# Cross-attention and routed experts on one core: table products summed over constants, and four weight sums at other ticks

## The reference

```python
scores = einsum('bsd,bmd->bsm', layernorm(x), ctx) / sqrt(512)
attn = softmax(where(mask, scores, -1e30)); readout = attn @ ctx       # zero where no row is allowed
x = x + readout
h = layernorm(x)
p = softmax(h @ G); value, indices = top_k(p, 2)                       # 8 experts
out = sum over the two: value * ((silu(h @ gate_e.T) * (h @ up_e.T)) @ down_e.T + (h @ lora_A_e.T) @ lora_B_e.T)
x = x + out
```

## Time and profile before

| | |
|---|---|
| median of 3 runs | 500.96 us (500.02 to 501.46) |
| profiled execution, its own time | 501.44 us |
| its span, first to last instruction | 499.6 us |
| mean granted TensorE clock | 0.995 |
| busy: TensorE, VectorE, ScalarE, GpSimd | 97%, 87%, 76%, 60% |

### The profile page before, as it was taken

One profiled execution on the slowest core, in us unless ns is written; L12 is line 12 of the kernel. 1 busy time (PEld: TensorE's weight loads), 2 busy tenths in 40 slices (PEclk: granted clock), 3 DMA queues, 4 the chain that ended last, 5 costly groups with the idle time before them and its releaser, 6 DMA issues.

```text
span 499.6 us, 16211 instructions
## 1 busy us (share of the span) xinstructions
PE 486.7 (97%) x4040; PEld 433.1 (87%) x4040; DVE 436.5 (87%) x1678; ACT 381.0 (76%) x1076; POOL 300.0 (60%) x440
## 2 busy tenths in 40 slices
PE   8999999999999989999999999999999999999994
PEld 7788888888888878899998999999998999999993
DVE  5799999999999987889988999999887888888885
ACT  4788888888888988888888778777565666666662
POOL 4327777777777887757886444445544445444544
PEclk9999999999999999999999999999999999999998
DMA  8999999999999999999999999989999999999932
GB/s 300 392 369 403 397 405 389 400 386 360 394 405 375 403 333 287 362 376 412 409 413 408 412 410 387 354 341 367 418 412 417 417 416 416 416 414 416 382 155 85
DMA packets 64839, 187.52 MB, mean 375 GB/s; under 512 B 9582, under 2 KB 9710, under 8 KB 64752
## 3 DMA queue, kind: packets, MB, share of 16 engines
q1 hardware_dynamic: 43584, 118.62, 62.6%
q0 software_dynamic: 20800, 67.65, 34.0%
q10 hardware_dynamic: 368, 0.21, 0.2%
HBM read 112.46 MB, written 78.73 MB: 383 GB/s over the span
## 4 chain that ended last, share of the span: by engine, by line
PE 73%; DMA 9%; POOL 6%; issue 6%; DVE 2%; ACT 2%; SPq 1%; POOLq 1%; DVEq 0%; ACTq 0%
PE rd L539 12%; PE bank L539 12%; PE bank L481 11%; PE bank L383 8%; PE rd L557 6%; PE rd L558 6%; PE rd L423 4%; DMA z_own<-z_rows 4%; PE bank L362 3%; PE rd L424 3%; DMA z_rows<-z_own 3%; PE rd L546 3%; POOL x_rows L1232 2%; DMA x_sb<-in_x 2%; PE rd L396 2%
## 5 line engine op out<-in xcount | busy, mean ns | idle before, releaser
L679 ACT COPY hT<-bank 128x512 f32<-128x512 f32 x140 | 81.7, 583 | 26.3 <-PE bank L481 22.2
L1232 POOL DMA_INDIRECT x_rows<-xe x64 | 65.7, 1026 | 32.4 <-issue 27.1
L539 PE MATMUL rd<-wg_sb,hT 128*128 x560 | 80.3, 286 | 0.4 <-ACT hT L679 0.4
L539 PE MATMUL bank<-wg_sb,hT 128*128 x560 | 80.2, 286 | 0.0
L383 PE MATMUL bank<-cc_sb,xnT 128*128 128x136 f32 x512 | 80.1, 286 | 0.0
L539 PEld LDWEIGHTS rd<-wg_sb,hT 128*128 128x128 f32 x560 | 72.6, 190 | 0.7 <-issue 0.7
L539 PEld LDWEIGHTS bank<-wg_sb,hT 128*128 128x128 f32 x560 | 72.6, 190 | 0.1
L383 PEld LDWEIGHTS bank<-cc_sb,xnT 128*128 128x128 f32 x512 | 68.3, 191 | 0.7
L557 PE MATMUL rd<-dn_a,ggT_a 128*128 x140 | 66.7, 477 | 0.6 <-DVE ggT_b L1119 0.4
L1248 POOL DMA_INDIRECT out_x<-z_shared x41 | 40.1, 979 | 40.0 <-DVE z_shared L1129 36.7
L1129 DVE SCALAR_TENSOR_TENSOR z_shared<-rd,z_shared 128x512 f32<-128x512 f32 x77 | 57.7, 749 | 1.9 <-PE rd L558 0.2
(11 more groups left out here) (187 smaller groups left out, 1192.4 us busy)
## 6 DMA issues: line engine op xcount, KB each, us to landing
cc_sb<-in_cc SPq DMA_DIRECT2D x64, 532.0 KB, 7.4
z_shared<-z_rows SPq DMA_DIRECT2D x41, 516.0 KB, 19.1
x_sb<-in_x SPq DMA_DIRECT2D x64, 256.0 KB, 6.5
z_own<-z_rows SPq DMA_DIRECT2D x29, 516.0 KB, 18.6
z_shared<-x_rows SPq DMA_DIRECT2D x36, 260.0 KB, 10.1
z_own<-x_rows SPq DMA_DIRECT2D x34, 260.0 KB, 10.9
z_rows<-pad SPq DMA_DIRECT2D x8, 516.0 KB
wg_sb<-in_wg SPq DMA_DIRECT2D x8, 288.0 KB, 6.3
```

Source lines behind the costliest of these rows:

```text
L539: mm = pe.matmul(gu_ps[q % 2][:, 0:GU], hT[:, q % 2, k, :], wg_flat[:, bass.ds(at + k * GU, GU)], start=(k == 0), stop=(k == KD - 1))
L679: act.copy(hT[:, q % 2, :, :], hT_ps[q % 2][:].rearrange("p (k s) -> p k s", k=KD)).then_inc(hT_ready, 1)
L1232: pool.indirect_dma_start(out=x1_rows[:, :], out_offset=rows_at(row, ROW1), in_=row, in_offset=None, bounds_check=ROWS - 1, oob_is_err=Fal ...
```

## The change

Four things change. `turn_table` issues one product instead of four: the weights are now a column of ones (`one_f`), and the moving operand is `table`, which has become 82 columns wide and holds the four numbers already multiplied by their constants; GpSimd multiplies (`table_words`, `table_rows`), and caps the rows in place in `jumps` (semaphore `capped`). `SUMS_AT` ends with 59, 60, 63, 64 instead of 57, 59, 61, 63 (index 12 to 15). `number(m)` moves from GpSimd's tick 4m + 7 to tick 4m + 8, behind the scatter there. TensorE's start waits for a second memset.

```diff
-SUMS_AT = sorted([*range(TB * 2 + 3, B, TB), B - 7, B - 3])
+SUMS_AT = sorted([*range(TB * 2 + 3, B, TB), B - 4, B])
...
-        expert, table, first_row = sb("expert", [2]), sb("table", [4]), sb("first_row", [2, NQ], I32)
+        expert, table, first_row = sb("expert", [2]), sb("table", [2 * (EARLY_GROUPS + NQ - KA)]), sb("first_row", [2, NQ], I32)
...
                 pe.wait_ge(table_ready, 2 * i + 2)
-                for k in range(4):
-                    what = const_sb[:, PACK + first:PACK + last] if k < 2 else ident[:, lo:hi]
-                    at = TABLES[i] + (k * (last - first) if k < 2 else 2 * (last - first) + (k - 2) * (hi - lo))
-                    mm = pe.matmul(rt_ps[:, at:at + what.shape[1]], table[:, k:k + 1].broadcast_to([P, P]), what, start=False, stop=True, skip_group_check=True)
+                n = 2 * (last - first) + 2 * (hi - lo)
+                mm = pe.matmul(rt_ps[:, TABLES[i]:TABLES[i] + n], one_f[:].broadcast_to([P, P]), table[:, 0:n], start=False, stop=True, skip_group_check=True)
                 mm.then_inc(tabT_done, 1)
...
-            pe.wait_ge(ones_set, 1)
+            pe.wait_ge(ones_set, 2)
             warm_up(WARM[0])
...
+            def table_words(i):
+                first, last = groups_of(i)
+                n = last - first
+                pool.tensor_tensor(table[:, 0:2 * n].rearrange("p (k q) -> p k q", k=2), spread(expert, n),
+                                   both(const_sb[:, PACK + first:PACK + last], n), ALU.mult).then_inc(table_ready, 1)
+
+            def table_rows(i):
+                (lo, hi), (first, last) = blocks_of(i), groups_of(i)
+                n, at = hi - lo, 2 * (last - first)
+                pool.wait_ge(capped, i + 1)
+                pool.tensor_tensor(table[:, at:at + 2 * n].rearrange("p (k q) -> p k q", k=2), spread(jumps, n),
+                                   both(ident[:, lo:hi], n), ALU.mult).then_inc(table_ready, 1)
+
             def early_table():
                 pool.wait_ge(tab_step, 15)
                 pool.tensor_tensor(jumps[:], jumps[:], row_at[:, :, 0], ALU.add).then_inc(tab_step, 1)
-                pool.tensor_scalar(table[:, 0:2], expert[:], 1.0, None, ALU.mult).then_inc(table_ready, 1)
+                table_words(0)
                 pool.wait_ge(tab_step, 16)
-                pool.tensor_scalar(table[:, 2:4], jumps[:], float(NOWHERE), None, ALU.min).then_inc(table_ready, 1)
+                pool.tensor_scalar(jumps[:], jumps[:], float(NOWHERE), None, ALU.min).then_inc(capped, 1)
+                table_rows(0)
...
             def overlap_rows():
                 pool.wait_ge(over_step, 5)
-                pool.wait_ge(table_ready, 4)
-                pool.tensor_tensor(over[:], over[:], table[:, 2:4], ALU.subtract).then_inc(over_step, 1)
+                pool.wait_ge(capped, 2)
+                pool.tensor_tensor(over[:], over[:], jumps[:], ALU.subtract).then_inc(over_step, 1)
...
             pool.memset(ones[:], 1.0).then_inc(ones_set, 1)
+            pool.memset(one_f[:], 1.0).then_inc(ones_set, 1)
...
+                if in_sweep(t, 8) and (t - 8) % TB == 0:
+                    number((t - 8) // TB)
...
                     gaps((t - 7) // TB)
                     turn_gaps((t - 7) // TB)
-                    number((t - 7) // TB)
```

More of the change, by code:

```diff
@@ L133, in xattn_moe @@
         ident = const_sb[:, IDENT:IDENT + P]
-        before, after, ones, tile_of = sb("before", [P], BF16), sb("after", [P], BF16), sb("ones", [P], BF16), sb("tile_of", [B], BF16)
+        before, after, ones, tile_of, one_f = sb("before", [P], BF16), sb("after", [P], BF16), sb("ones", [P], BF16), sb("tile_of", [B], BF16), sb("one_f", [1])
         base = sb("base", [2 * E], BF16)
@@ L206, in xattn_moe @@
             sem, ("strips_done", "strips_ready", "prod_done", "prod_ready", "part_ready"))
-        after_set, dn_hi_set = sem("after_set"), sem("dn_hi_set")
+        after_set, dn_hi_set, capped = sem("after_set"), sem("dn_hi_set"), sem("capped")
         top_ready, which_ready, pair_ready, gap_step, turn_step, lexp_ready, hot_ready = map(
@@ L1276, in early_jump, with spread, both @@
                 pool.tensor_tensor(jump[:, :, 0:E], jump[:, :, 0:E], past[:, :, 0:E], ALU.mult).then_inc(tab_step, 1)
+            def spread(what, n):
+                return what[:].rearrange("p (k o) -> p k o", o=1).broadcast_to([P, 2, n])
+            def both(rows, n):
+                return rows.rearrange("p (k q) -> p k q", k=1).broadcast_to([P, 2, n])
+            def table_words(i):
[9 more added lines that the diff above has]
+                                   both(ident[:, lo:hi], n), ALU.mult).then_inc(table_ready, 1)
             def early_table():
@@ L1335, in late_table @@
                 pool.tensor_tensor(jumps[:], jumps[:], row_at[:, :, 0], ALU.add).then_inc(tab_step, 1)
-                pool.tensor_scalar(table[:, 0:2], expert[:], 1.0, None, ALU.mult).then_inc(table_ready, 1)
+                table_words(1)
                 pool.wait_ge(tab_step, 42)
-                pool.tensor_scalar(table[:, 2:4], jumps[:], float(NOWHERE), None, ALU.min).then_inc(table_ready, 1)
+                pool.tensor_scalar(jumps[:], jumps[:], float(NOWHERE), None, ALU.min).then_inc(capped, 1)
+                table_rows(1)
             def overlap_bounds(i):
```

## The result

The changed kernel takes 503.86 us (median of 20 runs, 501.96 to 509.71) against 500.85 us for the kernel before in the same rounds; the ratio is 1.0044, 95% interval 1.0025 to 1.0063, so it is 1.3 to 3.2 us slower. The first profiled execution took 505.06 us, with a span of 503.3.

The account below looks back on a forecast made before the run. TensorE, busy 97% of the span, was taken as the bound. Waits for sums 2.94 us, less 0.38 for the late table, plus 1.4 for the clock, made 3.96 us on a 500.96 us median: 504.9 us, range 502.5 to 506.6.

Parts of the forecast that it names:

- The wait of ScalarE for sum 12: Tick 60: ScalarE's copy waits for GpSimd's sum, xnT behind it; TensorE's head of tick 61 comes 1.62 us later.
- GpSimd's pace: GpSimd, ticks 57 to 59: `x_scale` starts at 186.69, 0.79 us earlier; sum 12 starts at 192.42, ends at 193.70.
- The second pair: Sums 14 and 15: ScalarE's tick 64 waits for sum 14, making the softmax of tile 63 2.94 us late.
- The early table: First table product, before the wait for sum 12: 0.59 us saved on TensorE, taken by that wait, buys nothing.
- the late one: Late table product: 0.59 us saved on TensorE less some 0.2 us waiting for GpSimd's multiply, so 0.38 us.
- The clock: Granted clock falls in or just behind TensorE's 3.4 us gap, costing 1.4 us, bounds nothing to 3.2.
- (a): Rival: both stalls for sums come but the clock holds; 2.56 us slower, 503.5 us; chance 0.35.
- (d): The forecast itself: stalls for sums and a low clock, 504.9 us; chance 0.50.
- (b): Rival: only the first wait comes, sum 14 ending before ScalarE's tick 64 copy; 1.0 us, 502.0 us; chance 0.08.
- (c): Rival: sum 12 ready for ScalarE's copy, old stalls go, no new ones; -2.36 us, 498.6 us; chance 0.07.

Follow-up runs that it names:

- e2: Kernel before with only the last sums moved to ticks 59, 60, 63, 64, old table and row numbers: 505.25 us against 500.72, ratio 1.0101.
- e5: Changed kernel with GpSimd doing the sum before the scatter in ticks 59 and 63: 498.87 us against 500.79 for the kernel before, ratio 0.9947.
- the second profile: Profile of the changed kernel, unaltered, when run again beside other kernels: median 503.78 us against 500.79 for the kernel before, ratio 1.0066.
- e4: Changed kernel with the last sums at ticks 57, 60, 61, 64: 500.71 us against 500.72 for the kernel before, ratio 0.9995.
- e9: Kernel before with the new sum ticks and sum before scatter in ticks 59 and 63, old table and row numbers: 513.36 us against 515.04, slower chip.
- e10: e5 with GpSimd's inverse root also before the scatter in tick 58: 512.16 us against 515.04 for the kernel before, slower chip, ratio 0.9956.
- e1: Kernel before with only the new table products, sums and row numbers in their old places: 501.15 us against 500.72, ratio 1.0008.
- e6: Changed kernel with 26 products of ones behind the readout in TensorE's tick 60: 502.47 us against 500.79 for the kernel before, ratio 1.0036.
- e8: Changed kernel with its first pair of sums back, so ticks 57, 59, 63, 64: 501.52 us against 500.79 for the kernel before, ratio 1.0003.
- e7: Changed kernel, unaltered, run again beside other kernels: 503.78 us against 500.79 for the kernel before, ratio 1.0066.

## Why the prediction was right, step by step

I gave 504.9 us and a range of 502.5 to 506.6; it took 503.86. The mechanism held: both waits came where I said and for the reason that I gave. The size was somewhat too large. With the measured terms my sum is 2.72 - 0.63 = 2.1 us without the fall of the clock (I had 2.56) and 3.4 with it (I had 3.96), against 1.3 to 3.2 us by the ratio.

- **The wait of ScalarE for sum 12, with xnT behind it.** Right; e2 shows it without the table, e5 takes it away by the sum's place alone. I gave the head of tick 61 1.62 us more than before; counted from tick 57 it was 1.35 us (193.62 - 177.87 against 193.31 - 178.91) and 1.39 in the second profile. The wait that TensorE shows is 2.78 us and not 3.40. Of the difference 0.27 us is that the wait ended sooner than I had it, and 0.35 us that TensorE came to it later: ticks 57 and 58 were 0.21 us shorter than I had them, but tick 59 took 3.73 us instead of 3.36, and tick 60 3.00 instead of 2.81 up to the wait.
- **The 0.37 us of tick 59 is the step that I left out.** I checked the table against TensorE's need, but not `x_scale`, on which VectorE's copy of the table and mask step hang. In the trace of before this chain was met just in time. e4, e9 and e10 show it from three sides.
- **GpSimd's pace.** `x_scale` was to start 7.78 us after the head of tick 57 (186.69 less 1.04 and 177.87), and did 7.70 after; the sum was to start at 192.42 - 1.04 = 191.38, and did at 191.17. The step-by-step walk through the rows held to about 0.2 us. One of its steps was wrong: I kept the gap of 0.47 us ahead of the scatter behind the table, and it was 0.60.
- **The second pair.** Predicted 1.76 us on top of the shift at tick 62 (2.94 less 1.18). In the second profile, without a low clock, the shift at tick 62 was 1.17 us, and at the first gate product 2.72 us (31.65 less 28.93). So 1.55 us against 1.76: right to about 0.2 us.
- **The early table buys nothing, the late one counts.** The first half is right and wider than I said: I put it down to the wait for the sum, e1 and e9 show that it is lost without that wait too, since the wider table makes GpSimd 0.3 to 0.5 us later. For the late one I had a wait of 0.2 us; there is none, GpSimd was done a microsecond ahead, and the product takes 0.18 us instead of 0.81. The term was 0.38 and measured 0.63; in the whole time no run can tell it.
- **The clock.** It fell just behind the gap, as I said, and cost 1.34 us against the second profile of the same kernel (4.76 less 3.42) and 1.57 against e6, where I took 1.4, though I had put part of the low stretch into the gap and none lay there. But it didn't fall in every execution, and that I had not thought of: I had taken (a) and (d) for alternatives, and by the clocks of the runs they are two kinds of execution of one kernel, near 502.6 and 505.0 us. That the median came between my 503.5 and 504.9 is in part luck: it depends on how many runs had the fall. The Trainium skill's page "TensorE: Matmul & The Clock Gate" (section "Why this matters for your kernels") warns of idle gaps between bursts of matmuls. Two of the three profiles with a gap of 2.8 to 3.0 us agree with it; in the third nothing fell behind 2.80 us.
- **The rivals (b) and (c).** (b) did not happen: ScalarE waited 1.14 us for sum 14, and TensorE 0.99 and 0.53 us behind it. (c) did not happen, but e5 is (c) brought about by hand: I gave it 498.6 us, and it took 498.87.

## What to carry to other kernels

When a step is moved on one engine, look up where the engines of its neighbours stand at that time, not at their tick numbers: GpSimd was over a tick behind ScalarE, so a lead of one tick was a wait of 2.8 us, and ahead of the scatter in the same tick it was none. A saving on the bound engine counts only if no other engine is just in time there; the 0.6 us of the early table were given back within four ticks, because GpSimd's chain was nearly as long and the change had moved work onto it. And a stall of some microseconds on TensorE may cost half as much again through its clock: 1.3 to 1.6 us behind 2.8 to 3.0 here, in two profiles of three.

## What the runs showed of the hardware

The granted clock fell to 1.2 GHz behind a gap of 2.8 us between dense products in one profile of the changed kernel and stayed at 2.4 GHz behind the same gap in the other; behind two shorter waits (1.10 and 0.53 us, with one product between, e8) it fell as well, from about 207.3 to 210.7, while behind nearly the same two (0.97 and 0.53 us, e7) it stayed up. With products of ones in 1.6 us of the gap it stayed up in the one profile. The 26 of these took 1.61 us, 0.06 each, where the 44 of the warm-up at the kernel's start took 4.87 us, 0.11 each (kernel before), though the records give a granted clock of 1.00 for both. On one chip the kernels took 2 to 3% longer; for e5's kernel 9.6 of the 9.7 us of the span lie in the expert part, with pauses of ScalarE for which the profile mostly names nothing on the core.
